# A graph layer on one core: input tables laid out by the host, and the first stage's steps in another order

## The reference

```
h   = x @ W_in2f
Wij = (ssp(edge_attr @ Wf1 + bf1) @ Wf2 + bf2) * edge_weight     # ssp(v) = softplus(v) - log 2
m   = segment_sum(h[dst] * Wij, src, 50000)
m   = ssp(m @ Wo1 + bo1) @ Wo2 + bo2
out = layernorm(x + (x + m))                                      # over the 256 columns
```

## Time and profile before

| | |
|---|---|
| median of 3 runs | 1896.08 us (1895.0 to 1898.38) |
| the profiled execution, its own time | 1909.02 us |
| its span, first to last instruction | 1907.3 us |
| mean granted TensorE clock | 0.963 of full speed |
| busy: TensorE / VectorE / ScalarE / GpSimd | 92% / 84% / 78% / 76% |
| scatters, 392 of them | 1695 ns each |
| gathers, 392 of them | 982 ns each |
| moved by DMA | 363.35 MB |

### The profile page before, as it was taken

One profiled execution on the slowest core, in us unless ns is written; L12 is line 12 of the kernel. 1 busy time (PEld: TensorE's weight loads), 2 busy tenths in 40 slices (PEclk: granted clock), 3 DMA queues, 4 the chain that ended last, 5 costly groups with the idle time before them and its releaser, 6 DMA issues. The chain is left out here.

```text
span 1907.3 us, 37602 instructions
## 1 busy us (share of the span) xinstructions
PE 1752.6 (92%) x11780; PEld 1593.9 (84%) x11780; DVE 1599.3 (84%) x3760; ACT 1493.7 (78%) x2945; POOL 1452.6 (76%) x1385
## 2 busy tenths in 40 slices
PE   5999999999999988988988989889886999999996
PEld 4788888888888877877877878778776999999996
DVE  4888999999999977967967879769774999999996
ACT  4778888888888866866866867668664999999996
POOL 6422677787777777877777777777763999999998
PEclk9999999999999999989989999989897999999998
DMA  9999765666666665666656666666564999999995
GB/s 348 379 361 366 156 118 108 120 117 110 119 114 113 119 110 106 113 111 112 110 105 121 113 106 111 109 112 114 98 153 118 334 359 360 364 363 361 359 363 187
DMA packets 266063, 363.35 MB, mean 191 GB/s; under 512 B 126616, under 2 KB 178026, under 8 KB 265866
## 3 DMA queue, kind: packets, MB, share of 16 engines
q1 hardware_dynamic: 188902, 257.31, 41.7%
q0 software_dynamic: 75136, 102.45, 30.2%
q10 hardware_dynamic: 1828, 1.18, 0.2%
HBM read 206.71 MB, written 154.12 MB: 189 GB/s over the span
## 5 line engine op out<-in xcount | busy, mean ns | idle before, releaser
L364 POOL DMA_INDIRECT acc<-sums,src_ix x392 | 664.6, 1695 | 202.7 <-issue 144.4
L351 POOL DMA_INDIRECT xg<-in_x,dst_t x392 | 385.1, 982 | 193.9 <-issue 116.4
L817 DVE SCALAR_TENSOR_TENSOR m_l<-pair,wgt_t,m_h 128x256 fp32r<-128x256 f32 x392 | 171.6, 479 | 214.7 <-ACT m_h L649 214.7
L395 POOL TENSOR_SCALAR sums<-sums,neg_mean,rstd 128x256 f32<-128x256 f32 x392 | 283.1, 736 | 10.2
L781 DVE SCALAR_TENSOR_TENSOR same<-srcb,src_t,later 128x512 fp32r<-128x512 int32 (+3 forms) x392 | 288.3, 792 | 0.0
L649 ACT ACTIVATE m_h<-pair,wgt_t 128x256 fp32r<-128x256 f32 x392 | 164.7, 471 | 145.4 <-PE pair L426 125.7
L522 PE MATMUL pair<-m_h,same 128*128 128x256 f32 (+1 forms) x980 | 249.7, 289 | 1.7 <-ACT sums L656 1.7
L522 PE MATMUL pair<-m_l,same 128*128 128x256 f32 (+1 forms) x980 | 241.2, 281 | 0.0
L426 PE MATMUL pair<-wo_h,msg_h 128*128 128x256 f32 (+1 forms) x784 | 235.8, 301 | 3.8 <-DVE m_l L817 3.8
L426 PE MATMUL pair<-wo_h,msg_l 128*128 128x256 f32 (+1 forms) x784 | 227.1, 290 | 0.0
L426 PE MATMUL pair<-wo_l,msg_h 128*128 128x256 f32 (+1 forms) x784 | 226.6, 289 | 0.0
(11 more groups left out here) (109 smaller groups left out, 5480.5 us busy)
## 6 DMA issues: line engine op xcount, KB each, us to landing
acc<-fill SPq DMA_DIRECT2D x195, 256.0 KB
xg<-in_x SPq DMA_DIRECT2D x97, 512.0 KB, 6.8
sums<-acc SPq DMA_DIRECT2D x97, 512.0 KB, 7.3
out<-sums SPq DMA_DIRECT2D x97, 512.0 KB, 5.1
attr<-in_edge_attr SPq DMA_DIRECT2D x194, 128.0 KB
srcb<-in_src SPq DMA_DIRECT2D x97, 256.0 KB, 4.2
xg<-in_x,dst_t POOLq DMA_INDIRECT x392, 3.7
acc<-sums,src_ix POOLq DMA_INDIRECT x392
```

The costliest lines, as they stand in the source:

```text
L351: pool.indirect_dma_start(xg[0:g.p, g.xs, r], None, t["x"], bass.IndirectOffsetOnAxis(ap=dst_t[0:g.p, r, g.n:g.n + 1], axis=0)).then_inc(x ...
L364: pool.indirect_dma_start(acc, bass.IndirectOffsetOnAxis(ap=src_ix[g.slot][0:g.p, r:r + 1], axis=0), sums[0:g.p, g.slot, r], None, compute ...
L395: last = pool.tensor_scalar(normed[0:g.p, g.n % NRING, r], res[0:g.p, u, r], neg_mean[0:g.p, u, r:r + 1], rstd[0:g.p, u, r:r + 1], ALU.add ...
L817: dve.scalar_tensor_tensor(out=m_l[0:g.p, r], in0=bank[6][0:g.p, k * D:(k + 1) * D], scalar=col(wgt_t, r, g), in1=m_h[0:g.p, r].bitcast(F3 ...
```

## The change

1. The host hands src, dst and the weights over as tables, the attributes as a [64, 512] block for each group (the edges in the order r, then partition), the weights of the four products and bf1, bf2 as they lie in SBUF. With this `turn_a` and its bank use go: `a_high` and `a_low` read the loaded attributes from SBUF. TensorE's first transposes, VectorE's casts and copies of the tables and the separate tails go.
2. wo2 is loaded behind the first stage's loads into an attribute buffer, and rounded and split when the first stage's lists are through. bo1, bo2, wf1, ones share memory with `sums`.
3. Rings: RING 11 to 12, XRING 8 to 11, ARING and SRING 3 to 2; AHEAD 20 to 23. Clears: 8, then SyncE waits for the first gathered tile, then up to 36, then 16 a group.
4. The lists of TensorE, ScalarE and VectorE. The compare is four stages now, `compare(0)` to `compare(3)`, one operation each.

```diff
-RING = 11
-XRING = 8
-ARING = 3
-SRING = 3
-AHEAD = 20
-FIRST_CLEARS = 24
-CLEARS_A_STEP = 15
+RING = 12
+XRING = 11
+ARING = 2
+SRING = 2
+AHEAD = 23
+EARLY_CLEARS = 8
+FIRST_CLEARS = 36
+CLEARS_A_STEP = 16
...
             def load_attr(n):
                 g, u = group(n), n % ARING
-                wait(sp, at_ps, n - ARING + 1)
+                wait(sp, al_sb, n - ARING + 1)
                 for k in range(2):
-                    sp.dma_start(attr[0:g.p, u, :, k, :], rows_of(t["edge_attr_64"], g).rearrange("(p r) a -> p r a", r=R)).then_inc(attr_in[u], 16)
+                    sp.dma_start(attr[k * A:(k + 1) * A, u], t["edge_attr_64"][n]).then_inc(attr_in[u], 16)
...
+            sp.dma_start(dst_t[:].rearrange("p r g -> p (r g)"), t["dst"].rearrange("p r g -> p (r g)")).then_inc(dst_in, 16)
             load_attr(0)
+            sp.dma_start(bo1, t["L0_gnn_bo1"].partition_broadcast(P)).then_inc(bo1_in, 16)
...
+            clear_to(EARLY_CLEARS)
+            sp.wait_ge(xg_in[0], 16 * R)
             clear_to(FIRST_CLEARS)
...
+            wait(sp, al_sb, G - ARING + 1)
+            sp.dma_start(wo2, t["L0_gnn_Wo2"]).then_inc(wo2_in, 16)
...
-            run((w_of(1), 2), (turn_a, 0), (summed(0), 3), (h_of(0), 1), (summed(1), 3), (filter1, 0), (turn_x(0), 0),
-                (out1(0), 2), (turn_x(1), 0), (w_of(0), 1), (h_of(1), 1), (out1(1), 2), before={1: filter_bias})
+            run((w_of(1), 2), (h_of(0), 1), (summed(1), 3), (out1(0), 2), (filter1, 0), (out1(1), 2), (turn_x(0), 0),
+                (w_of(0), 1), (turn_x(1), 0), (h_of(1), 1), (summed(0), 2), before={1: filter_bias})
...
             def a_high(g):
-                act.wait_ge(at_ps, g.n + 1)
+                act.wait_ge(attr_in[g.n % ARING], (g.n // ARING + 1) * 32)
                 wait(act, z_ps, g.n)
-                high(a_h[:, :, 0:g.p], bank[2][:].rearrange("f (r e) -> f r e", r=R)[:, :, 0:g.p], ah_sb)
+                high(a_h[:, :, 0:g.p], attr[:, g.n % ARING].rearrange("f (r e) -> f r e", r=R)[:, :, 0:g.p], ah_sb)
...
-            run((keep_y(0), 4), (msg_high(1), 3), (ssp_high(0), 2), (ssp_high(1), 2), (keep_h(0), 2), (absolute(0), 1),
-                (absolute(1), 1), (expo(0), 1), (m_high(0), 3), (keep_y(1), 4), (expo(1), 1), (x_high(0), 1), (loga(0), 1),
-                (loga(1), 1), (x_high(1), 1), (keep_h(1), 2), (m_high(1), 3), (a_high, 0), (msg_high(0), 2), before={1: weights})
-
+            run((keep_y(0), 3), (ssp_high(0), 1), (ssp_high(1), 1), (a_high, 0), (msg_high(1), 2), (keep_h(0), 1), (keep_y(1), 3),
+                (m_high(0), 2), (absolute(0), 0), (absolute(1), 0), (expo(0), 0), (m_high(1), 2), (x_high(0), 0), (expo(1), 0),
+                (loga(0), 0), (msg_high(0), 1), (x_high(1), 0), (keep_h(1), 1), (loga(1), 0), before={1: weights})
+
+            act.wait_ge(wo2_in, 16)
+            act.wait_ge(h_ps, G * H)
+            act.activation(wo2_h[:], wo2, ACT.Copy).then_inc(wo2_cast, 1)
...
-            run((m_low(0), 3), (message(0), 2), (x_low(0), 1), (softplus(0), 1), (softplus(1), 1), (x_low(1), 1),
-                (m_low(1), 3), (message(1), 2), (a_low, 0), (msg_low(0), 2), (target, 3), (msg_low(1), 2), (ssp_low(0), 1),
-                (ssp_low(1), 1), (compare, 2), before={1: first_weights, 2: tables, 3: second_weights})
-
+            run((softplus(1), 1), (message(1), 2), (a_low, 0), (ssp_low(0), 1), (msg_low(1), 2), (ssp_low(1), 1), (target, 2),
+                (compare(0), 1), (compare(1), 1), (m_low(0), 2), (compare(2), 1), (compare(3), 1), (m_low(1), 2), (message(0), 1), (x_low(0), 0),
+                (msg_low(0), 1), (softplus(0), 0), (x_low(1), 0), before={0: biases, 1: first_weights, 3: second_weights})
+
+
+            dve.wait_ge(wo2_cast, 1)
+            low(wo2_l[:], wo2, wo2_h[:], wo2_made)
```

More of the change, by code:

```diff
@@ L150, in build @@
         CLEAR = 2
-        fill = sb("fill", [P, 4, D])
-        attr = sb("attr", [P, ARING, R, 2, A])
+        fill = sb("fill", [P, CLEAR, D])
+        attr = sb("attr", [P, ARING, ROWS])
         srcb = sb("srcb", [P, SRING, ROWS], I32)
@@ L234, in build, with xg_count @@
         CLEARS = N // P // CLEAR
-        TABLES = 4 + R
+        TABLES = 1 + R
         assert N // P % CLEAR == 0
+        CLEAR_REST = len(range(CLEARS * CLEAR * P, N + R * P, CLEAR * P))
         def rows_of(ap, g):
             return ap[bass.ds(g.n * ROWS, g.rows)]
-        def last_of(ap):
-            for k in range(G - MAIN):
-                rows = ROWS if MAIN + k < G - 1 else TAIL
-                yield k, rows // R, ap[(MAIN + k) * ROWS:(MAIN + k) * ROWS + rows].rearrange("(p r) -> p r", r=R)
+        def xg_count(g):
+            return sum(16 * R for n in range(g.xs, g.n + 1, XRING))
         def col(table, r, g):
@@ L347, in stage @@
                 def stage(g):
-                    if g.n == 0:
-                        pool.wait_ge(dst_made, 2)
-                    wait(pool, xt_ps, (g.n - XRING + 1) * 2)
+                    if g.n == 0 and r == 0:
+                        pool.wait_ge(dst_in, 16)
+                    if r == 0:
+                        wait(pool, xt_ps, (g.n - XRING + 1) * 2)
                     pool.indirect_dma_start(xg[0:g.p, g.xs, r], None, t["x"],
@@ L405, in _ @@
             pe.wait_ge(made, 6)
-            for b, rows, arrived, count, done in ((5, dst_f, dst_cast, 1, dst_ps), (6, src_f, rows_cast, 1, tab_ps), (7, wgt_f, rows_in, 16 * 2, tab_ps)):
-                pe.wait_ge(arrived, count)
-                for r in range(R):
-                    last = pe.transpose(bank[b][:, r * MAIN:(r + 1) * MAIN], rows[0:MAIN, r::R], ident[0:MAIN, 0:MAIN])
-                last.then_inc(done, 1)
             def filter_bias():
@@ L439, in turn_x @@
                 return stage
-            def turn_a(g):
-                pe.wait_ge(attr_in[g.n % ARING], (g.n // ARING + 1) * 32)
-                wait(pe, ssp_sb, g.n * H)
-                for r in range(R):
-                    last = pe.transpose(bank[2][:, r * P:r * P + g.p],
-                                        attr[0:g.p, g.n % ARING, r].rearrange("e k a -> e (k a)"), ident[0:g.p, 0:g.p])
-                last.then_inc(at_ps, 1)
             def filter1(g):
@@ L600, in stage @@
                     if g.n == 0:
-                        act.wait_ge(b_in, 16 * 4)
+                        act.wait_ge(b_in, 16 * 2)
                     act.wait_ge(z_ps, g.n + 1)
@@ L783, in compare @@
                                              accum_out=alike[0:g.p, g.par, a:a + 1]).then_inc(same_ready, 1)
+                return stage
             def target(g):
```

169 lines of the change are left out of this document (77 added, 92 removed).

## The result

| | changed kernel | kernel before | ratio, 95% interval |
|---|---|---|---|
| median of 4 runs | 1982.53 us (1973.87 to 1985.46) | 1895.59 us (1895.0 to 1898.38) | 1.0448 [1.0413, 1.0483] |
| profiled execution, span | 1984.06, 1982.3 us | 1909.02, 1907.3 us | |

The forecast was 1900 with a range of 1866 to 1928: it was 83 us short. Its likeliest case had the sign right, but by +3 us, less than the 4 us that it called the least that can be told. The changed kernel was run again in two later sessions (a session is a batch of runs made together), each beside the kernel before. It took 1967.44 us against 1903.67 (1.0338) in one and 1930.17 against 1909.62 (1.0107) in the other. Part of the loss comes and goes between sessions with the program unchanged, and that part is what the prediction lacked.

The account below looks back on a forecast made before the run. GpSimd bounds the old first stage; afterwards the 14.4 us lap binds. First stage 178 + 1238 + 35.5 = 1452 us, +3; span 1907.3 + 3 = 1910, profiled 1912, median 13 lower, 1899, called 1900; range 1866 to 1928.

Parts of the forecast that it names:

- likeliest case: Whole run: lap 14.3 to 14.6 us, start 172 to 184, time 1885 to 1915 us; chance 0.50.
- GpSimd's load: First stage: 12 more gathers ahead of the first scatter bring GpSimd from 12.82 to 12.75 us a group.
- The landing wait: GpSimd's wait for the last scatter to land may shrink: bounded by 0 and 0.57 us in 76 groups, 43 us.
- The rule weighed from the Trainium skill: VectorE operations with two SBUF inputs, now also a_low, can hold GpSimd's shared port and lengthen scatters; sum left unchanged.
- The lap: First stage: the dependent round through VectorE, ScalarE and TensorE from softplus(1) to softplus(1) takes 14.4 us a step, was 13.09.
- Rival 1: First stage: GpSimd remains the bound, if the step is under 14.1 us; 24 us less, 1872 us; chance 0.22.
- rival 3: First stage: scatters meeting VectorE's compares make GpSimd slower than the lap, 13.33 us a group; 1927 us; chance 0.10.
- From there nine steps of 14.4 and little more: group 11 at 178 (bounds 167, ..., and 185): Start: from group 2's turn of x at 46 us, nine steps bring group 11's to 178 us; before, 172.38.
- Then 86 x 14.4 = 1238: First stage, group 11 to 97: 86 steps of 14.4 us take 1238 us, so group 97 is turned at 1416.
- Rival 2: First stage: the lap is longer through semaphore waits or TensorE's clock; 14.7 to 15.1 us, 1925 to 1960 us; chance 0.18.
- The median runs 13 below the profiled execution: Whole run: the profiled 1912 us less 13 gives a median of 1899 us.
- Tail and second stage: After group 97's turn of x, 35.5 us empty the pipe (before 39.5); the second stage stays at 458.4 us.

Follow-up runs that it names:

- e1: Changed kernel with the kernel before's lists of TensorE, ScalarE and VectorE (less turn_a), compare as four stages; 1865.3 us, ratio 0.9797.
- e11: e1's kernel with the gathers of groups 3 to 22 spread evenly and clears as 8, 24, then 20 a group; 1858.53 us, ratio 0.9777.
- e3: Changed kernel with a_high first in ScalarE's list instead of fourth; 1918.76 us, ratio 1.0076.
- e16: Changed kernel with both turn_x before out1(1), a_high behind msg_high(1), a_low behind ssp_low(0) and msg_low(1); 1850.26 us, ratio 0.9689.
- e18: Changed kernel run again unedited, in session six; 1930.17 us, ratio 1.0107.
- e6: Changed kernel with XRING 8 and AHEAD 20 instead of 11 and 23; 1950.63 us.
- e8: Changed kernel where the gathers of groups 3 to 10 each wait until the group three before is turned; 1983.05 us.
- e9: Changed kernel with the gathers of groups 3 to 22 spread evenly, by a wait that grows from group to group; 1978.39 us.
- e13: Changed kernel with only one group of gathers a step from group 3 on, and AHEAD 15 instead of 23; 1951.66 us.
- e14: Changed kernel run again unedited, as control in session five; 1967.44 us against 1903.67 for the kernel before.
- e12: Changed kernel with groups 3 to 10 loaded by 32 plain DMAs of SyncE instead of GpSimd's indirect DMAs; 1937.18 us.
- e17: e12 run again, in session six; 1937.74 us.
- e10: Changed kernel where GpSimd, before each group's first scatter, waits until the gather issued last has landed; 2060.56 us.
- e5: Kernel before with the new order of the three engines alone, loads, clears and rings as before; 1995.84 us, ratio 1.0504.
- e15: New loads, old order, one group of gathers a step from group 3 on, AHEAD 17, clears 8, 24, then 20 a group; 1897.07 us.
- e7: Changed kernel with no clear before the loads of group 4, then 18 a group; 1981.82 us.

## Why the prediction was wrong

- **The bound before** (GpSimd): e1 and e11 confirm it. With the new loads and the old order GpSimd binds again, 12.1 us a group, and the kernel is 2% faster than before.
- **GpSimd's load.** The landing wait went nearly as far as its bound had it, and the scatters got shorter: 12.1 to 12.2 us a group instead of 12.8 (the bound gives 12.3), scatters 1663 ns in the mean after 1695. The rule weighed from the Trainium skill ("SBUF — State Buffer", section "SBUF: two separate sides") would have lengthened the scatters through a_low; no such lengthening shows in the mean. That section limits the case of two SBUF inputs to GpSimd operations that read SBUF, and tells of waiting descriptors for VectorE's two-port modes; the prediction joined the two. The compares became cheaper, which I had not seen: 546 ns after 792 in the mean. It changed nothing, since m_low(0) is reached nearly as late through TensorE (6.50 in the working). That this place of the lap still came out is luck.
- **The lap.** Right to 0.05 us (14.44 for 14.4), place by place, and e3 and e16 shift it by moving steps. Rival 1 (GpSimd binds) fell, rival 3 too.
- **"From there nine steps of 14.4 and little more: group 11 at 178 (bounds 167, ..., and 185)"** is the first step that failed: 215.7. Where nothing stalls (e18) it is 192.0. Of these 14 us 4 are the attribute tile, which came at 49.87 and not at 46. Some 9 are the way from there to turn_x of group 2, at 58.97: both halves of out1 now stand ahead of it in TensorE's list, with the wait between them, which the working left out (in the kernel before it is 4.8 us). The other 24 us are the stalls by late signals of TensorE, which the trace of before doesn't show at all.
- **"Then 86 x 14.4 = 1238"** is the second, and failed in size: 1272.4 measured, 30 us of it in long steps, the rest is 14.44 for 14.4. The term for delays of single signals was nothing. Rival 2 named a longer lap by waits and by the clock, at 0.18, and its 14.7 to 15.1 holds the measured mean of 14.80; but it priced it evenly, per step, and with nothing for the start. What came were single delays of up to 2.2 us that the lap passes on in full and the clock enlarges: between 230 and 850 us late signals of 17 us in sum made the steps 30 us longer. The old order takes up part of such delays: in e1, over the same stretch, 24 us of them made the steps 15 us longer.
- **"The median runs 13 below the profiled execution"** failed: 1.5 below, 11 us of the 83. The two numbers of the kernel before were probably of different sessions. Its profiled 1909.02 us at a clock of 0.963 fits sessions four and six (medians 1909.61 and 1909.62, clocks 0.961 to 0.964), where nothing stalls, better than the medians of 1895 to 1904 of the others, and its trace has no late signal. That it is so isn't shown: single runs of the other sessions reach 1912.65.
- **Tail and second stage**: right to 0.2 us.
- **The range.** From the lap and the later start alone, without any stall, the changed kernel is 1930 us where the kernel before is 1910: +21 us, which from 1896 would be 1917, inside the range. The range held no term for delays that the trace of before could not show: not one signal of TensorE that ended a wait in it is late.

Shown: the order's lap, the price of the order, that clears and full DMA engines are not what stalls the start, that the stall follows GpSimd's runs of gathers (e6, e8, e9, e13 against e14), and that stalls and long steps are the same thing to the engines, a late signal of TensorE. In the traces of before, e12, e16, e17 and e18 no wait was ended by such a signal; in all others 4 to 34 were, by one of over 1 us. The long steps go with GpSimd running ahead: there are none in e10 up to 940 us, and in the eleven traces with the new order that have them the last one begins before GpSimd first waits over 1 us for sums (794 and 830 us in the changed kernel, 1116 and 1165 in e3). Open: what ties TensorE's late signals to GpSimd's indirect DMAs, and why not in every session. The same runs stall nobody in session six (e16 and e18). The run of 48 gathers without a stall in the kernel before (6.98 to 69.5 us) says little, as its trace was probably taken in such a session; e5, e1 and e11 stall with the old loads or the old order.

## What to carry to other kernels

With a list per engine written by hand, the step is the longest lap through the lists, not the busiest engine: add it up from softplus to softplus, and move what lies on it. An order without slack turns every delay of one engine, of whatever cause, into time of the whole, and a gap of 3 us in TensorE costs once more through its clock; so leave a stage of slack or give the range a term for it. Don't issue long runs of indirect DMAs while other engines must start up: where signals came late, one group a step brought the start 29.5 us forward and the end 15.8 (e13 against e14). The smaller lead that goes with it has its price where GpSimd binds (e15, 1897 us, against 1865 of e1 in another session). And run the control again in the session of the experiment, and the trace with the times: one conclusion (e12) was a session, not an edit, and so, it seems, were the 13 us between profile and median. When a wait ends in "remote" or "issue", compare the end of the work that it waits for with the time at which the semaphore was raised.

## Not expected of the hardware

- While GpSimd issued gathers back to back, signals of TensorE came up to 43 us behind the end of their matmuls, and VectorE stood idle for up to 48.9 us (e1), or 40.5 with the DMA engines only 35% busy (e7); eight gathers in a row made a step of 14.4 us one of 20 (e9). Signals of VectorE and ScalarE were not late, in any trace.
- The same program took 1982.5, 1967.4 and 1930.2 us in three sessions, while the kernel before took 1895.6, 1903.7 and 1909.6: not in the same direction.
- VectorE's compare of 512 int32 columns took 0.75 us with columns in order, and 1.15 before, when the edges' src were read with a stride of four elements.
- TensorE's granted clock was 0.50 over the 2.7 us after one gap of 3.16 us, and 1.00 after gaps of 0.98.
